# GpSimd waits for a small write of its own behind every gather, and each pair's result is stored by one transfer

## The reference

```python
proj    = einsum('bchw,oc->bohw', x, Wc) + bc          # 1x1 convolution, 256 -> 256
flows   = einsum('bchw,koc->kbohw', x, Woff) + boff    # 4 heads, 2 offsets each
weights = softmax(einsum('bchw,kc->bkhw', x, Wwt) + bwt, axis=1)
feats   = grid_sample_bilinear_zeros(proj, base + flows)   # one sampled image per head
out     = x + einsum('kbohw,bkhw->bohw', feats, weights)
```

## Time and profile before

| what | value |
|---|---|
| time, median of 3 runs (lowest to highest) | 712.29 us (709.59 to 715.42) |
| span of the profiled execution | 712.8 us |
| PE busy | 612.1 us (86%) |
| DVE busy | 550.0 us (77%) |
| POOL busy | 363.5 us (51%) |
| ACT busy | 362.1 us (51%) |
| DMA, software queue (the gathers, for the most part) | 43488 packets, 154.55 MB, 59.0% of 16 engines' span |
| DMA, hardware queue (SP's transfers) | 33836 packets, 42.03 MB, 17.0% |

### The profile page before, as it was taken

One profiled execution on the slowest core, in us unless ns is written; L12 is line 12 of the kernel. 1 busy time (PEld: TensorE's weight loads), 2 busy tenths in 40 slices (PEclk: granted clock), 3 DMA queues, 4 the chain that ended last, 5 costly groups with the idle time before them and its releaser, 6 DMA issues.

```text
span 712.8 us, 10744 instructions
## 1 busy us (share of the span) xinstructions
PE 612.1 (86%) x3020; PEld 488.4 (69%) x3029; DVE 550.0 (77%) x1316; ACT 362.1 (51%) x892; POOL 363.5 (51%) x385
## 2 busy tenths in 40 slices
PE   1999799999997897798989797978979977888888
PEld 0444475778886776586868686867868866676777
DVE  6999774579998739595789685969687859786796
ACT  0298885789985442352443654335364426234242
POOL 0030593235554475465656565656665655556640
PEclk9999899999999567797999998999998999899999
DMA  9900001127777798799999999999999998999992
GB/s 358 369 22 1 0 1 54 44 84 210 211 211 237 243 371 303 291 354 387 358 352 364 381 345 376 346 360 373 364 379 360 358 371 301 367 394 360 368 368 60
DMA packets 77366, 197.04 MB, mean 276 GB/s; under 512 B 7337, under 2 KB 36812, under 8 KB 77196
## 3 DMA queue, kind: packets, MB, share of 16 engines
q0 software_dynamic: 43488, 154.55, 59.0%
q1 hardware_dynamic: 33836, 42.03, 17.0%
HBM read 168.05 MB, written 28.51 MB: 276 GB/s over the span
## 4 chain that ended last, share of the span: by engine, by line
PE 40%; DVE 10%; issue 10%; another core or an unknown queue 5%; ACT 2%; POOL 0%; DVEq 0%
PE ps L1534 24%; PE ps L1559 7%; DVE ps L1164 5%; PE ps L1561 4%; PE ps L1484 2%; PE ps L1547 2%; ACT v L1311 1%; DVE ps L1161 1%; DVE wvs L1171 0%; DVE wvs L1164 0%; DVE xs L1178 0%; DVE wq L1171 0%; PE ps L1594 0%; DVE wq L1164 0%
## 5 line engine op out<-in xcount | busy, mean ns | idle before, releaser
L954 POOL DMA_INDIRECT v<-table,index x252 | 236.2, 937 | 151.4 <-issue 62.8
L1534 PE MATMUL ps<-v 128*128 128x256 f32 x786 | 209.3, 414 | 35.9 <-issue 28.0
L1164 DVE SCALAR_TENSOR_TENSOR ps<-v,weights,ps 128x256 f32<-128x256 f32 x489 | 215.3, 486 | 2.6 <-DVE ps L1161 1.0
L1534 PEld LDWEIGHTS ps<-v 128*128 128x128 f32 x786 | 157.4, 209 | 67.2 <-issue 37.3
L1311 ACT ACTIVATE v<-ident,weights 128x128 f32<-128x128 f32 x464 | 139.2, 388 | 8.7 <-remote 5.9
L1324 ACT COPY pick_mask<-ps 128x512 f32<-128x512 f32 x18 | 10.5, 585 | 133.4 <-remote 84.6
L1403 PE MATMUL ps<-wq,s_ring 128*128 128x256 f32 x288 | 68.1, 380 | 1.5 <-ACT ps L1247 0.9
L941 POOL TENSOR_TENSOR xs<-xs,v 128x512 f32<-128x512 f32 x36 | 45.1, 1276 | 46.6 <-DVE v L1011 46.6
L1324 ACT COPY sample<-ps 128x512 f32<-128x512 f32 x17 | 10.0, 585 | 114.6 <-remote 73.7
L1403 PEld LDWEIGHTS ps<-wq,s_ring 128*128 128x128 f32 x288 | 53.9, 191 | 9.4 <-issue 2.9
L488 ACT ACTIVATE a_ring<-xs,small 128x768 f32<-128x768 f32 x48 | 49.0, 1026 | 10.2 <-POOL t_ring L475 5.2
(11 more groups left out here) (174 smaller groups left out, 971.2 us busy)
## 6 DMA issues: line engine op xcount, KB each, us to landing
table<-stage SPq DMA_DIRECT2D x72, 256.0 KB, 3.2
xs<-in_x_dram SPq DMA_DIRECT2D x11, 768.0 KB, 11.3
out_dram<-xs SPq DMA_DIRECT2D x28, 256.0 KB
v<-table,index POOLq DMA_INDIRECT x252
early<-const_syn POOLq DMA_DIRECT2D x18, 192.0 KB, 3.8
ana<-const_ana SPq DMA_DIRECT2D x1, 2304.0 KB, 20.0
out_dram<-xs SPq DMA_DIRECT2D x7, 238.0 KB
stage<-table,index POOLq DMA_INDIRECT x36
```

The source lines that it names most:

```text
L954: nc.gpsimd.indirect_dma_start(places[a], None, table, bass.IndirectOffsetOnAxis(ap=index[:, t, k:k + 1], axis=0)) \
L1164: V.scalar_tensor_tensor(to, corner, weight, ps[:, DVE_SUM, i * C:(i + 1) * C], ALU.mult, ALU.add).then_inc(added, 1)
L1534: m = T.matmul(ps[:, PE_SUM[i], 0:C], diag[2 * u + i][n], places[a][:, q * C:(q + 1) * C], start=n == 0, stop=n == len(mine) - 1)
```

## The change

Behind every gather, POOL writes zero into a column of a new tile `pause` (128 partitions, one element each) and waits until that write is complete before it goes on. This is 288 writes and 288 waits. The seven stores that were two transfers become one transfer over all 128 rows each, and the last wait of SP counts 36 transfers instead of 43.

```diff
+                pause = sb3("pause", [P, NT, HEADS])
+                paused = sem("paused")
...
-                FEWER = (slice(0, 119), slice(119, P))
-                ON_FEWER = range(4, LAST, 5)
...
                         for p in range(LAST):
                             sp.wait_ge(out_ready, p + 1)
                             here = slice(p * 2 * P, (p + 1) * 2 * P)
-                            for rows in FEWER if p in ON_FEWER else (slice(0, P),):
-                                sp.dma_start(out_c[rows, :, here], xs[rows, :, here]).then_inc(written, 16)
+                            sp.dma_start(out_c[:, :, here], xs[:, :, here]).then_inc(written, 16)
...
-                        sp.wait_ge(written, 16 * (PAIRS + 1 + len(ON_FEWER) * (len(FEWER) - 1)))
+                        sp.wait_ge(written, 16 * (PAIRS + 1))
...
                                 nc.gpsimd.indirect_dma_start(places[a], None, table,
                                                              bass.IndirectOffsetOnAxis(ap=index[:, t, k:k + 1], axis=0)) \
                                     .then_inc(landed[a], 16)
+                                nc.gpsimd.memset(pause[:, t, k:k + 1], 0.0).then_inc(paused, 1)
+                                pool.wait_ge(paused, t * HEADS + k + 1)
```

## The result

The changed kernel takes 723.63 us (median of 4 runs, 720.44 to 724.94), the kernel before on the same chip 712.77 us (709.59 to 715.42). The ratio is 1.0129, with a 95% interval of [1.0079, 1.018]. The prediction said 699 us with a range up to 722: it was wrong in size and in sign. Some executions of a kernel are in a slower state; the medians here are over all executions, while the ratios and their intervals are worked out from those outside it, so a ratio is not the quotient of two medians. Five later jobs ran on five chips, called 8, 5, 7, 10 and 9 here in the order of the jobs; that of this first comparison has no number.

What follows compares the result with a forecast made beforehand. DMA and PE were near their limits, with PE's signals late while POOL issues gathers. 712.8 - 14 (DMA at 370 GB/s) + 0.4 (first tile's pauses) = 699 us, less 0.5 to the median, rounded 699; range 685 to 722.

Steps and rivals of the forecast that it cites:

- the chained rows: Profile rows of a small POOL operation with a wait and a transfer behind it, giving a 0.31 us gap.
- the 0.61 us: Gap behind a gather on POOL at which its idle cover is gone, a period of 1.55 us a gather.
- PE's late signals: Gather stage: PE's signals arrive 5 to 12 us late while POOL issues gathers back to back; ACT, DVE and POOL wait.
- PE's signals come through between gathers: Gather stage: with the pause the long stalls go and DMA bounds it, 14 us less.
- Rival 1: Gather stage: nothing changes, signals stay late and POOL's waits swallow the pauses; about 713 us, chance 0.28.
- the cover: POOL from 290 to 690 us: 81 us of true waits hide the 34 us of added pauses.
- 370 GB/s: DMA rate forecast for the gather stage, halfway between 358 and the best window's 381; 426 us instead of 440.
- Rival 2: POOL becomes the pace as the gap behind a gather grows beyond 0.61 us; about 725 us, chance 0.15.
- Rival 3: Even stores cost: engines spared by the two-part stores now finish last, up to 6.4 us; about 719 us, chance 0.07.
- ACT's unknown waits at L1324: Sign: ACT's copy waits for a releaser the profile couldn't identify, to fall from 158 us to under 60.
- PE's idle time without a cause at L1534: Sign: PE's 29.2 us idle there, with no cause in the profile, to fall by half.
- the bias copy: Sign: DVE's copy L1142 at the stage's start, waiting for PE's bias products, to come near 257 us, not 268.

Runs made afterwards that it cites:

- pause_192_again: Kernel before plus a 128x192 memset and a wait behind every gather, repeated on chip 10: 699.32 us, ratio 1.048.
- pause_only: Kernel before plus only the 128x1 memset and wait behind every gather, stores still in two parts, on chip 8: 722.97 us, ratio 1.0106.
- store_only: Kernel before with only the seven two-part stores made single 128-row transfers, no memset or wait, on chip 8: 716.44 us, ratio 1.0009.
- before_again: The kernel before, unchanged, measured once more on chip 9: 669.01 us (14 runs).
- half_bytes: Kernel before with each gather bringing one table row per pixel instead of two, half the bytes, on chip 5: 710.66 us, ratio 0.9961.
- pause_128: Kernel before plus a 128x128 memset and a wait behind every gather, on chip 7: 715.84 us, ratio 1.0004.

## Why the prediction was wrong

**The steps that held.** The memset takes 0.11 us (0.10 predicted). The period is 1.32 us (1.37 predicted from the chained rows; the gap behind the memset is 0.27, not 0.31). POOL's gap stays below the 0.61 us from which it would be the pace, and that limit, 1.55 us a gather, was about right for a late chip: at 1.54 the excess is gone. Without late signals it lies lower, at 387.7 / 287 = 1.35 us, and pause_192_again is over it. The stores cost nothing on chip 8, as taken. PE's late signals were real, and what goes with them was the largest loss of the kernel: with plain transfers on chip 5, or on a chip without them, it takes 666 us.

**The step that failed: "PE's signals come through between gathers".** I took releases within 2 us of POOL's silence for proof that a little silence helps, but the pause leaves 0.38 us between gathers, not 2. With the pause the lateness is 2.35 us in the median (2.32 before), summed over 35 copies 92 us (100 before), and the unknown waits of ACT and DVE in the whole run are 283 us (247 before; single executions scatter, with 244 us in pause_only and 221 in store_only). They are gone at a period of 1.54 us on chip 5 and still there at 1.485 us on chip 7. The DMA rate from 290 us on fell from 359 to 352 GB/s where 370 was forecast. The term was -14 us and is 0. Rival 1 had this step right ("lets nothing through") and argued for it with the gaps of 0.30 us that did not help either.

**The second failed step, shared with rival 1: the cover.** "POOL's 81 us of waits swallow the 34." The pauses were 287 x 0.08 = 23 us, and the waits took only 15 of these; the stage grew by 8 us, 442.0 to 450.0, and the median by 10.9. On chip 9 the same 23 us are swallowed whole, the excess falling from 32 to 7. My reading is that on a late chip POOL's waits are holds, not slack: when the signal comes, PE and DVE are short of data and wait through the burst, which is then longer by 0.08 us for each gather. The traces don't bear this out: in both of the first chip no wait of PE or DVE in the stage names a transfer's landing, where before_again has 33 and 42 us of them. They don't refute it either, as 138 us of these two engines' waits have no known cause in the kernel before. What is shown is that the pause costs on the first chip and on 8 and doesn't on 9, where no signal is late; that the late signals make the difference, and nothing else in which the chips differ, is likely but was only argued, and so is how a hold passes the cost on.

**Sizes.** Had the signals been on time, the gain would have been 44 us, not 14: I took 370 GB/s between a mean and a best window of 381, but those windows lay between holds themselves, and the same gathers run at 411 GB/s on chip 9. A DMA share of 0.97 did not mean that DMA was near its limit: half_bytes takes as long with 0.66.

**The rivals.** Rival 2's time (725 us) is near what was measured, but not by its mechanism: the gap is 0.38 us with the memset, well under 0.61, and 71 us of excess remain. Rival 3 is ruled out by store_only on chip 8, where DMA was hardly the bound. The Trainium skill's rule on the count of engines (DMA: Bandwidth & Descriptors, section "Why a DMA increments its semaphore by 16 and not by 1") and that on the slower engines 7 and 15 (same page, section "Latency and other measured facts") would have made the even stores cost or gain; the run on chip 8 shows neither beyond 0.4%. The first rule alone, 16 engines in place of 7 and 9, does not speak against the change, as the prediction had it; only the second does.

**What would show it.** I had named ACT's unknown waits at L1324 as the sign (158 us to under 60). They fell to 152. PE's idle time without a cause at L1534 fell from 29.2 to 26.9 us where half was forecast. Of the signs of on-time signals only the bias copy came as told, near 257 us. The first sign was a poor one: ACT waits there 188 to 195 us between 290 and 690 us in chip 9's traces too, with PE named as the releaser. The end of the producer against the start of the consumer is the better one. I also set the sum 0.5 us above the median; the changed kernel's profiled execution has a time of 723.65 us beside a span of 721.2, so the time lies 2.4 us over the span, and the span of 712.8 belongs to a run of about 715.

**What stays open.** Why some chips deliver these signals late, whether the signals alone are late or PE's work and its recorded ends too, and what in an indirect gather brings it about (plain transfers at the same period ran on chip 10 only, where nothing is late). Whether that is a lasting trait of a chip or a condition at the time: each chip was seen in one job. On chip 9 the ratio makes 4.7 us; of the 7.8 us between the spans of the two traced executions 4.4 us lie ahead of the first gather, where nothing was changed (the first gather starts at 245 to 248 us in some traces and at 249 to 250 in others, whatever the kernel), 1.7 us between the first gather and the last, and 1.7 us behind it. Whether the pause or the even stores bring the gain wasn't tried on such a chip.

## What to carry to other kernels

Don't count wait time on an engine as cover for added work before you know that its releaser is itself on time. Compare the end of the producer with the start of the consumer first: where a known pair is microseconds apart, the wait is a symptom, and how much it covers has to be measured. Here 23 us of pauses lengthened the stage by 8 us, and the 54 us of pause_128 cost nothing. Before tuning against such a delay, run the kernel on several chips: a pause that gained 1.2% on one lost 4.8% on another, and the change of this study lost 1.3% on one and gained 0.7% on another.

## What the runs showed of the hardware that I had not expected

- One kernel runs in 666 to 669 us on two chips and in 710 to 717 us on three others and in the first comparison. Where it was traced at 669 us, every copy of ACT starts 0.04 us after PE's last transpose ends; in the first comparison the median is 2.3 us and the largest 8.2 us.
- On a chip with late signals, 128 rows of 4 KB gathered by indices cost POOL 0.94 us and the lateness, the same bytes as a plain transfer 0.53 us and none (0.04 us), and the latter ran 6.4% faster.
- 16 DMA engines moved 411 GB/s over most of the stage on chip 9, at a share of 1.03; 381 GB/s at a share of 1.00 on the first chip was no limit.
- A POOL memset of 128x1 behind a gather is free in the gap of 0.30 us behind it; waiting for it makes the gap 0.27 us behind the memset, 0.08 us more in all. The Trainium skill's rule that a POOL write completes only once all eight cores have landed (GPSIMD Engine Reference, section "Instruction dispatch") showed as no longer wait than that.
